# A norm's root moved to GpSimd and its scaling to ScalarE, zero products on TensorE, and stages in another order

## The reference

```
x = x + attn(ln(x))      # per-token head mixing: q.k over 16 heads, softmax over the heads, times v
x = x + ffn(ln(x))       # 2 experts, top 1: silu(x w_gate) * (x w_up), then w_down
x = x + ssm(ln(x))       # delta = softplus(...), h[t] = exp(delta A) h[t-1] + delta x B, y = C h + x D
x = x + moe(ln(x))       # 64 experts, top 6, capacity 64, and a shared expert of width 352
```

## Time and profile before

| | |
|---|---|
| median of 3 runs | 665.01 us (660.06 to 665.32) |
| profiled execution, its own time | 664.68 us |
| its span, first to last instruction | 662.9 us |
| TensorE busy | 555.4 us, 84% |
| VectorE busy | 512.9 us, 77% |
| ScalarE busy | 191.9 us, 29% |
| GpSimd busy | 128.2 us, 19% |
| mean granted TensorE clock | 0.92 of full |

### The profile page before, as it was taken

How to read it: one execution, slowest core, us unless ns; L and a number is a source line. 1 busy time by engine, 2 the same in 40 slices (tenths; PEclk the granted TensorE clock), 3 DMA queues, 4 the chain that set the end, 5 groups by cost and what they waited for, 6 DMA issues and landing times.

```text
span 662.9 us, 7383 instructions
## 1 busy us (share of the span) xinstructions
PE 555.4 (84%) x2313; PEld 341.1 (51%) x2313; DVE 512.9 (77%) x1182; ACT 191.9 (29%) x372; POOL 128.2 (19%) x121
## 2 busy tenths in 40 slices
PE   5688999889999779879799757665899899999954
PEld 4564666534667356565465643434575344434543
DVE  6998898164899968989999998999988466456535
ACT  1122321226443254432643305222111223223100
POOL 2120210210002000002000110000000577677600
PEclk9799999787999959989899876778999999999979
DMA  7950000317301192001730207397192499995588
GB/s 281 409 194 28 33 16 18 111 33 278 136 1 64 40 331 93 0 33 32 255 129 1 80 24 256 129 354 273 45 306 81 122 354 354 347 341 96 63 301 340
DMA packets 62740, 105.74 MB, mean 159 GB/s; under 512 B 6096, under 2 KB 51920, under 8 KB 62192
## 3 DMA queue, kind: packets, MB, share of 16 engines
q1 hardware_dynamic: 51792, 85.97, 37.0%
q0 software_dynamic: 8608, 17.21, 10.2%
q10 hardware_dynamic: 2304, 2.10, 0.9%
HBM read 79.80 MB, written 25.46 MB: 159 GB/s over the span
## 4 chain that ended last, share of the span: by engine, by line
DVE 40%; PE 31%; DMA 15%; issue 6%; ACT 5%; SPq 1%; POOL 1%; DVEq 0%; POOLq 0%; ACTq 0%
DMA part_rows<-bc,att_s 11%; DVE scan_area L1363 9%; PE misc_ps L755 5%; PE gate_ps L738 5%; DVE scan_area L1366 5%; DVE scan_area L1359 5%; PE up_ps L738 4%; DMA bc<-part_rows 3%; DVE sig L1303 3%; PE turn_ps L676 2%; DVE front_area L1308 2%; PE ssm_ps L697 2%; PE gate_ps L830 2%; PE up_ps L830 2%; DVE ln_st L1116 1%
## 5 line engine op out<-in xcount | busy, mean ns | idle before, releaser
L1363 DVE TENSOR_TENSOR_SCAN scan_area<-scan_area 128x1024 f32<-128x1024 f32 x32 | 73.3, 2292 | 6.2 <-ACT scan_area L1037 2.3
L755 PE MATMUL misc_ps<-big,front_area 128*128 x288 | 71.3, 404 | 4.7 <-ACT front_area L937 3.0
L738 PE MATMUL gate_ps<-big,front_area 128*128 x144 | 72.0, 624 | 2.8 <-ACT front_area L937 2.8
L973 ACT ACTIVATE sig<-gate_ps 128x512 f32<-128x512 f32 (+1 forms) x48 | 28.6, 596 | 139.8 <-PE up_ps L738 89.6
L738 PE MATMUL up_ps<-big,front_area 128*128 x144 | 68.3, 597 | 0.0
L755 PEld LDWEIGHTS misc_ps<-big,front_area 128*128 128x128 f32 x288 | 58.3, 205 | 19.4 <-issue 11.0
L661 POOL DMA_INDIRECT part_rows<-bc,att_s x32 | 50.4, 1576 | 21.7 <-DMA part_rows<-bc,att_s 14.6
L1303 DVE SCALAR_TENSOR_TENSOR sig<-sig,gate_ps 128x512 f32<-128x512 f32 (+1 forms) x48 | 32.7, 682 | 24.6 <-issue 16.5
L1037 ACT ACTIVATE scan_area<-scan_area,a_col 128x511 f32<-128x511 f32 x64 | 42.0, 714 | 28.9 <-DVE scan_area L1363 24.8
L632 POOL DMA_INDIRECT front_area<-ysorted_dram,slot_idx x16 | 20.0, 1251 | 154.1 <-DMA ysorted_dram<-front_area 150.4
L738 PEld LDWEIGHTS up_ps<-big,front_area 128*128 128x128 f32 x144 | 28.0, 195 | 35.9 <-issue 35.9
(11 more groups left out here) (274 smaller groups left out, 941.0 us busy)
## 6 DMA issues: line engine op xcount, KB each, us to landing
bc<-bc_dram SPq DMA_DIRECT2D x4, 4096.0 KB, 14.0
big<-in_wgu SPq DMA_DIRECT2D x14, 704.0 KB
part_rows<-zeros SPq DMA_DIRECT2D x16, 512.0 KB, 15.6
front_area<-in_wgu SPq DMA_DIRECT2D x6, 704.0 KB
scan_area<-in_wgu SPq DMA_DIRECT2D x6, 704.0 KB
big<-part_rows SPq DMA_DIRECT2D x8, 512.0 KB, 6.4
big<-in_wd SPq DMA_DIRECT2D x12, 256.0 KB
table<-row_area SPq DMA_DIRECT2D x4, 640.0 KB, 3.3
```

What stands on the lines that cost most here:

```text
L738: mm = pe.matmul(bank[:], xs_t[:, k, j, :], gu0[:, expert_of[b, j], k, g, half * 512:(half + 1) * 512], start=(k == 0), stop=(k == K - 1))
L755: mm = pe.matmul(misc_ps[:, 0:D], h0_t[:, half, c * P:(c + 1) * P], dn0[:, expert_of[b, j], half * 4 + c, :], start=(half == 0 and c == 0) ...
L1363: nc.vector.tensor_tensor_scan(buf.rearrange(flat), d_a[:, g % 2, :, :].rearrange(flat), buf.rearrange(flat), 0.0, ALU.mult, ALU.add).then ...
```

## The change

Three things are done at once.

1. For the normalisations 2 (all batches) and 3 (batches 0 to 2) VectorE stops after the first guess. GpSimd computes the root in twelve small operations on 128x4 tiles, ending with -mean * r, and ScalarE scales the four tiles as `x * r + (-mean r)`.
2. A new stage `warm` is one product with zeros of 256 columns into the bank that TensorE's next turn will use, behind the same wait as that turn; there are 34 of them. There are 28 `awake` stages (two products each) before and after.
3. The list `plan` holds the same stages otherwise, in another order.

```diff
--- before.py
+++ after.py
@@ -70,6 +70,8 @@
 
 ROOT = 9
 LN = 3 * J + ROOT
+NORM_STATS = 2 * J + 2
+ROOT_STEPS = 12
 AT_DIFF, AT = 5, 10
 RT_SEL, RT_DIFF = J + 1, J + 2
 RT_OPS = [J + 11, J + 17, J + 23, J + 27]
@@ -200,7 +202,7 @@
 
         ln_st = [sb(f"ln_st{i}", [P, J, 6]) for i in range(4)]
         ln_mv = [sb(f"ln_mv{i}", [P, J, 2]) for i in range(4)]
-        ln_w = [sb(f"ln_w{i}", [P, 3, J]) for i in range(4)]
+        ln_w = [sb(f"ln_w{i}", [P, 3 + (i >= 2), J]) for i in range(4)]
 
 
         xn_f = in_front["xn_f"].rearrange("p (j d) -> p j d", j=J)
@@ -321,6 +323,8 @@
         silu_steps = sem("silu_steps")
         y_copied = sem("y_copied")
         ln_steps = [sem(f"ln_steps{i}") for i in range(4)]
+        root_steps = [sem(f"root_steps{i}") for i in (2, 3)]
+        rows_normed = [sem(f"rows_normed{i}") for i in (2, 3)]
         attn_steps = sem("attn_steps")
         attn_exp = sem("attn_exp")
         route_steps = sem("route_steps")
@@ -383,43 +387,46 @@
 
 
         plan = """
-            ffn_load.0.0 attn_in.0.0 awake.0.0 attn_turn.0.0 awake.0.1 attn_in.1.0 attn_qkv.0.0 attn_qkv.0.1 attn_in.2.0
...
+            awake.0.0 attn_in.0.0 attn_in.1.0 attn_turn.0.0 ffn_load.0.0 warm.0.0 attn_qkv.0.0 attn_qkv.0.1 attn_qkv.0.2
...
 
         def stage_of(name, batch, part="0"):
             return name, int(batch), int(part)
@@ -632,8 +639,46 @@
                     pool.indirect_dma_start(xs[b % 2][:, j, :], None, ysorted_dram[b > 0],
                                             bass.IndirectOffsetOnAxis(slot_idx[:, b, j:j + 1], 0)).then_inc(yt_loaded, 16)
 
+            def root_of(n, b):
+                s, w, done = root_steps[n - 2], ln_w[n], b * ROOT_STEPS
+                v, t, r, u = (w[:, row, :] for row in range(4))
+                tt, ts = nc.gpsimd.tensor_tensor, nc.gpsimd.tensor_scalar
+                pool.wait_ge(ln_steps[n], (b + 1) * NORM_STATS)
+                tt(t, r, r, ALU.mult).then_inc(s, 1)
+                pool.wait_ge(s, done + 1)
+                tt(t, t, v, ALU.mult).then_inc(s, 1)
+                pool.wait_ge(s, done + 2)
+                ts(u, t, -10.0 / 3.0, None, ALU.add).then_inc(s, 1)
+                pool.wait_ge(s, done + 3)
+                tt(t, t, u, ALU.mult).then_inc(s, 1)
+                pool.wait_ge(s, done + 4)
+                ts(u, t, 5.0, None, ALU.add).then_inc(s, 1)
+                pool.wait_ge(s, done + 5)
+                tt(r, r, u, ALU.mult).then_inc(s, 1)
...
+                ts(u, t, -0.5 / CUBE ** 3, 1.5 / CUBE, ALU.mult, ALU.add).then_inc(s, 1)
+                pool.wait_ge(s, done + 9)
+                tt(r, r, u, ALU.mult).then_inc(s, 1)
+                ts(t, ln_mv[n][:, :, 0], -1.0, None, ALU.mult).then_inc(s, 1)
+                pool.wait_ge(s, done + 11)
+                tt(v, t, r, ALU.mult).then_inc(s, 1)
+
+            def ssm_norm(b, _):
+                root_of(2, b)
+
+            def gates_in(b, _):
+                if b < B - 1:
+                    root_of(3, b)
+
+            def last_rows_normed(b):
+                return (rows_normed[1], (b + 1) * J) if b < B - 1 else (ln_steps[3], b * NORM_STATS + LN)
+
             def gates(b, _):
-                wait_apart(pool, passed["pool"], (gate_steps, (b + 1) * GT), (ln_steps[3], (b + 1) * LN))
+                wait_apart(pool, passed["pool"], (gate_steps, (b + 1) * GT), last_rows_normed(b))
                 nc.gpsimd.tensor_copy(xf[:, :, D:XW], sc66[:, :, 0:E]).then_inc(scores_copied, 1)
 
 
@@ -681,7 +727,12 @@
                 for j0 in range(0, tiles, 2):
                     if normed:
                         n, b = normed
-                        pe.wait_ge(ln_steps[n], (b + 1) * LN - J + j0 + 2)
+                        if n < 2:
+                            pe.wait_ge(ln_steps[n], (b + 1) * LN - J + j0 + 2)
+                        elif (n, b) == (3, B - 1):
+                            pe.wait_ge(ln_steps[n], b * NORM_STATS + LN - J + j0 + 2)
+                        else:
+                            pe.wait_ge(rows_normed[n - 2], b * J + j0 + 2)
                     if after_ssm is not None:
                         pe.wait_ge(x_after_ssm, (after_ssm + 1) * K)
                     transposes([((jj * K + k) * P, P, P, src[:, j0 + jj, k * P:(k + 1) * P])
@@ -695,6 +746,11 @@
                     pe.wait_ge(x_after_ssm, B * K)
                 for _ in range(2):
                     pe.matmul(ssm_ps[:, 0:D], ident[:], zeros[:, 0:D], start=True, stop=True)
+
+            def warm(b, _):
+                slot, use = turn.k % 2, turn.so_far()
+                pe.wait_ge(turn_moved, use - 1)
+                pe.matmul(turn_ps[slot][:, 0:D], ident[:], zeros[:, 0:D], start=True, stop=True)
 
             def attn_turn(b, _):
                 if b == 0:
@@ -986,6 +1042,15 @@
             def ffn(b, s):
                 half_tanh(P, 1)
 
+            def apply_norm(n, b, dst):
+                act.wait_ge(root_steps[n - 2], (b + 1) * ROOT_STEPS)
+                for j in range(J):
+                    nc.scalar.activation(dst[:, j, 0:D], x_res[:, b * J + j, :], ACT.Identity, bias=ln_w[n][:, 0, j:j + 1],
+                                         scale=ln_w[n][:, 2, j:j + 1]).then_inc(rows_normed[n - 2], 1)
+
+            def ssm_norm(b, _):
+                apply_norm(2, b, xn_s)
+
             def ssm_in(b, _):
                 if b == 0:
                     act.wait_ge(w_ssm_loaded, 16 * 5)
@@ -1038,6 +1103,8 @@
                                          scale=a_col[:, c, n0 + n:n0 + n + 1]).then_inc(da_ready, 1)
 
             def gates_in(b, _):
+                if b < B - 1:
+                    apply_norm(3, b, xf)
                 move_tiles(back_t if b == B - 1 else gate_t[b], J)
 
             def gates_turn(b, _):
@@ -1111,20 +1178,29 @@
 
             def norm(n, b, dst):
 
-                s, w, mv = ln_steps[n], ln_w[n], ln_mv[n]
+                norm_root(n, b, norm_stats(n, b) + 2 * J)
+                for j in range(J):
+                    if (n, b) != (3, B - 1):
+                        apply_norm(n, b, dst, j)
+
+            def norm_stats(n, b):
+
+                s, w, mv, first = ln_steps[n], ln_w[n], ln_mv[n], b * (LN if n < 2 else NORM_STATS)
                 for j in range(J):
                     nc.vector.bn_stats(ln_st[n][:, j, :], x_res[:, b * J + j, :]).then_inc(s, 1)
-                wait_apart(dve, passed["dve"], (s, b * LN + J))
+                wait_apart(dve, passed["dve"], (s, first + J))
                 for j in range(J):
                     nc.vector.bn_aggr(mv[:, j, :], ln_st[n][:, j, :]).then_inc(s, 1)
-                dve.wait_ge(s, b * LN + 2 * J)
+                dve.wait_ge(s, first + 2 * J)
                 ts(w[:, 0, :], mv[:, :, 1], EPS, None, ALU.add).then_inc(s, 1)
-                dve.wait_ge(s, b * LN + 2 * J + 1)
-
-
+                dve.wait_ge(s, first + 2 * J + 1)
+                ts(w[:, 2, :].bitcast(I32), w[:, 0, :].bitcast(I32), -0.5, float(HALF_EXPONENT), ALU.mult, ALU.add
+                   ).then_inc(s, 1)
+                return first
+
+            def norm_root(n, b, root):
+                s, w = ln_steps[n], ln_w[n]
                 v, t, r = (w[:, row, :] for row in range(3))
-                root = b * LN + 2 * J
-                ts(r.bitcast(I32), v.bitcast(I32), -0.5, float(HALF_EXPONENT), ALU.mult, ALU.add).then_inc(s, 1)
                 dve.wait_ge(s, root + 2)
                 tt(t, r, r, ALU.mult).then_inc(s, 1)
                 dve.wait_ge(s, root + 3)
@@ -1140,9 +1216,6 @@
                 dve.wait_ge(s, root + 8)
                 stt(out=r, in0=t, scalar=1.5 / CUBE, in1=r, op0=ALU.add, op1=ALU.mult).then_inc(s, 1)
                 dve.wait_ge(s, root + ROOT)
-                for j in range(J):
-                    if (n, b) != (3, B - 1):
-                        apply_norm(n, b, dst, j)
 
             def apply_norm(n, b, dst, j):
 
@@ -1321,7 +1394,7 @@
 
             def ssm_norm(b, _):
                 wait_from_one(dve, group_summed, b * GROUPS)
-                norm(2, b, xn_s)
+                norm_stats(2, b)
 
             def ssm_proj(b, _):
                 if b == 0:
@@ -1374,7 +1447,10 @@
 
             def gates_in(b, _):
                 wait_apart(dve, passed["dve"], (table_stored, b * 16))
-                norm(3, b, xf)
+                if b < B - 1:
+                    norm_stats(3, b)
+                else:
+                    norm(3, b, xf)
 
             def gates(b, _):
                 _, use = misc.next()
```

## The result

The changed kernel takes 677.24 us, median of 3 executions (671.58 to 680.85), against 665.01 before: a ratio of 1.0228, 95% interval 1.0158 to 1.0298. It is slower, where 659.5 was forecast; whether by more than 2% the interval leaves open. Ratios leave out executions more than 1.5% above the fastest of the same kernel, and need not be the quotient of the medians beside them (here 1.0184). The profiled execution is the shortest of the three, 671.58 us, so the profiles show 6.9 of the 12.2 us; the experiments had to find the rest.

The account below looks back on a forecast made before the run. VectorE's work and the latency from normalisation to delta were taken as two close limits. Terms 0 + 0 + 0.8 - 0.3 - 1.7 - 3.9 = -5.1 us took the profiled 664.68 us to 659.6, stated as 659.5, range 648 to 669.

Parts of the forecast that it names:

- Two limits close together: Scan of the four batches: VectorE's work and the latency from normalisation to delta both bound the kernel.
- The 18.7 us: Seven normalisations: VectorE work removed, 2.7 us each, giving 646 us if every microsecond counted.
- -4.3 us for the last groups: Fourth ffn_out to the end of the last scan group: this piece was forecast 4.3 us shorter.
- rival (b): Root on GpSimd: quick at 0.20 us a step, and the clock holds; 651 us, chance 0.22.
- (a): Root on GpSimd: held at each step while VectorE works, mean step 0.73 us; 675 us, chance 0.14.
- four paths: Roots on GpSimd: about four of the seven lie on the path, each root 2.9 us longer.
- Must be scaled, turned and moved before the functions start at 19: Third batch: gates_in.1.0, its root ending at 16.4 us, precedes ScalarE's functions, so delta starts at 22.2 us.
- this batch's sum: Third batch: delta 1.8 us later, less two selection rounds done earlier before, summed to -0.3 us.
- the credit for two selection rounds: Third batch: two rounds that were done earlier before were credited at 2 x 1.06 us.
- ffn_out behind one more pair: Start: first ffn_out queued behind another pair of gate operations; the stretch summed to 0, between -3 and +2 us.
- the cover: Zero products on TensorE: its own waiting hides their 14.6 us; uncovered, 2 to 3 us would reach VectorE's path.
- the rule weighed in the prediction: GpSimd's root: two-SBUF-input VectorE instructions and GpSimd instructions reading SBUF exclude each other, possibly holding a root twelve times.

Follow-up runs that it names:

- the fillers: Kernel before with 16.8 us of useless VectorE work, in two versions: among the scans 678.95 us (1.0261), ahead of delta 673.11 us (1.0125).
- root_twice: Changed kernel with twelve more dependent GpSimd steps in each of the seven roots: 700.57 us, ratio 1.0513.
- functions_first: Changed kernel with ScalarE's ssm_exp.2 and ssm_exp.3 listed ahead of gates_in.1 and gates_in.2: 689.02 us, ratio 1.0300.
- root_on_vector: Changed kernel with root and -mean*r computed on VectorE in eight steps, ScalarE still scaling: 672.41 us, ratio 1.0066.

## Why the prediction was wrong

**What bounds the kernel: right, and drawn too weakly.** "Two limits close together" is what the fillers show, but they follow each other in a batch: the latency from `ffn_out` to delta wherever VectorE waits there (all batches but the third), VectorE's work from delta on. The 18.7 us were all taken from the first part. In three batches of the kernel before VectorE waited there already, and in the third the function that delta needs (ScalarE, L1016) was done at 325.53 us, 3.05 us ahead of delta at 328.58:

```profile
324.49 1.04 ACT L1016 ACTIVATE scan_area<-scan_area 128x1024 f32<-128x1024 f32 x1
```

So with a chain no longer than before the freed work could bring delta forward by about 3 us in one batch and not at all in the others. The prediction priced that batch by batch but kept -4.3 us for the last groups, of which -2.7 came.

**The root: its size wrong in the change's favour, its weight wrong against it.** A step takes 0.29 us, not 0.38, half way to rival (b)'s 0.20; (a) did not occur. The added 2.3 us (3.4 and a start of 0.25 against 1.4) were counted on four paths. `root_twice` shows seven, at about 1 us for 1 us of root.

**The step that failed most is the third batch's.** "Must be scaled, turned and moved before the functions start at 19" allowed 2.6 us from the root's end for this; it took 5.5 (327.32 to 332.86), for the scaling is 0.52 us a tile and had to wait for the projection's move, and the turn stood behind three zero products at the lower level. Delta came 24.1 us after the end of `ffn_out`, not 22.2. That is 1.9 of the 5.3 us by which this batch's sum was off (+5.0 for -0.3). Another 2.1 is the credit for two selection rounds: in the kernel before they stand in the second batch (301.60 and 302.71 us), so in the third they are added work that fills the wait, and spare nothing behind it. The last 1.3 lies behind delta, where 59.65 us pass for 58.39 with about as much VectorE work. Over the whole batch VectorE is busy for 3.3 us less and idle for 8.2 us more. `functions_first` shows that delta's lateness alone is not the cost: with delta 4.7 us earlier this batch was 1.2 us shorter. The second batch came much as forecast (delta at 20.4 for 20.2, +1.5 for +0.8), but its waits were priced too low: 0.74 to 3.53 us for the squares, +2.8 for +1.9, and the half block's wait of 6.08 us it had only as a later delta.

**The start: ffn_out behind one more pair was priced at 0 and cost 4.2 us,** 2.0 of which came back in the first batch. The prediction saw the pair, and that the gain from `ffn_down.0.4` is bounded by the load, but not that the wait for this load would lower the clock for just the products that the pair hangs on.

**The zero products: the cover was right (they cost nothing), the benefit was not.** 34 of them left the falls behind the waits of the norm path. Filling those took the changed kernel from 1.0228 to 1.0103.

**What the 2.3% are made of.** Filling gains in the kernel before too, so a kernel with filled waits is to be compared with 0.9947, not with 1. With the waits as they are, the list (with its zero products) and the scalings on ScalarE cost 0.7% (1.0066) and the root on GpSimd 1.6% more. With filled waits list and scalings cost 1.0% (1.0050 against 0.9947) and the root 0.5% more (1.0103), and the intervals of the last two overlap. So a part of what the root costs may be the clock's, which falls behind the waits; that a longer root makes it fall is a guess that no run tests, and the difference between 1.6 and 0.5% is hardly more than the intervals. The root's cost is shown by `root_on_vector` and `root_twice`; the order with the scalings, 0.7 to 1.0%, no run took apart further. The 1.9 us behind `tables` were not followed up: that piece varies from 152.3 to 157.4 us over kernels that do the same there.

## What to carry to other kernels

Ask of work taken off the fullest engine in which piece it stands: if the engine waits at the end of that piece for a chain through other engines, the work is free already, and what counts is the chain; if it does not wait, look how far ahead the chain is, since that is all that can be won. Price an offload by the chain's length and by everything queued behind the helper on its engine, and follow a moved stage through every engine's list, since the wait can come back two engines on. Fill the waits of a chain that feed slow products, not waits at large.

## What the runs showed of the hardware

- GpSimd's dependent operations on 128x4 tiles start 0.27 to 0.32 us apart (0.19 to 0.24 us each), in all seven roots, beside VectorE's gate operations and selection rounds too.
- The copy of `gates` (0.40 us) is held by VectorE, but not by the scan, as the prediction had it: in every profile with a copy of 1.45 us it starts 0.03 to 0.04 us behind a product of two SBUF tiles of 1.23 us and ends 0.25 to 0.27 us behind that product, as at 428.43 us in the earlier trace rows, where VectorE has

```profile
428.39 1.22 DVE L1359 TENSOR_TENSOR scan_area<-scan_area,bc 128x1024 f32<-128x1024 f32 x1
```

  Beside such a product of 0.69 us it took 0.91 or 0.92, and beside operations with one input in PSUM 0.39 to 0.41. In the changed kernel no step of a root ran beside a VectorE product of two SBUF tiles, so the rule weighed in the prediction stays untested for them.
- A wait of 1.7 to 2.1 us on TensorE behind full work was followed within 4 us by products at the 1.2 GHz level in eight of nine profiles; with the wait filled to 0.67 to 0.75 us they ran at 2.4 GHz in three of three. In the ninth, `root_on_vector`, the same 1.75 us did not lower the clock, so the wait does not decide alone; single executions of one program differ by 1 to 2%.
- ScalarE's Identity with scale and bias over 128x256 takes 0.52 us, VectorE's 0.35 us.
